# Expert weight parts: the load of part n+1 issued ahead of the stores of part n

## Chip, core and metric

The kernel runs on one core of one Trainium2 chip. The metric is device time in microseconds (us) for one execution. All engines of the core (TensorE, VectorE or DVE, ScalarE or ACT, GpSimd or POOL, SyncE or SP) run their own instruction streams and meet at semaphores.

## The reference

Four layers run one after the other on 3125 nodes of 256 features, each added to its input:

```python
x = x + gcn(_layernorm(x), edges, edge_weight, ...)     # 2 GCN layers
x = x + moe(_layernorm(x), ...)                         # 8 experts, top 2 of each token
x = x + ggnn(_layernorm(x), edges, edge_weight, ...)    # 5 rounds of message passing and a GRU
x = x + ffn(_layernorm(x), ...)                         # 8 experts, 2 chosen for all
```

There are 50000 edges. In a GCN layer a node sums the rows of its neighbours, weighted by the edges; the expert layer of the second line is what the change touches:

```python
xe = xn[None, :, :] * ln_g[:, None, :] + ln_b[:, None, :]
h = gelu(einsum('end,edh->enh', xe, W1) + b1[:, None, :])      # W1: 8 x 256 x 1024
y = einsum('enh,ehd->end', h, W2) + b2[:, None, :]             # W2: 8 x 1024 x 256
```

## The kernel before

**Dense planes.** The sparse sums are made dense. The kernel holds two matrices of 3200 x 3200 in device memory, `plane_a` (for the GCN) and `plane_w` (for the GRU rounds). They are filled with zeros (and ones on the diagonal of `plane_a`), and the edges are added to them by scatters of GpSimd with accumulation: 392 per plane, each of 128 edges. For `plane_a` they go in 28 batches of 14 (`NB`, `G`; L495 to L499, called from the loop at L508). A batch starts only when the one before has landed (L515); from batch 9 on, one scatter into `plane_w` (L501 to L505) is issued at its head. When the 28 batches are out, GpSimd goes on with `plane_w` alone, up to 252 of its 392, and does the rest between the gathers of the MoE layer.

**Split weights.** TensorE computes in a format of reduced precision, so each operand is given as a rounded high half and the rest as a low half, and a product takes three matmuls (L605). The weights of the first expert layer are brought into this form early: 16 parts (`PARTS`), W1 and W2 of 8 experts, each part 128 partitions x 2048 fp32 (1 MB). SyncE loads a part into `part_in` (`load_part`, L341 to L345), ScalarE rounds it into `part_hi` (`round_part`, L951 to L955), VectorE subtracts to get `part_lo` (`rest_of_part`, L1383 to L1387), and SyncE stores both halves to `w_split` in device memory (L356 to L358). All three buffers have two places, taken by n % 2. `round_part` waits for the load (`part_got`) and, from n = 2, for the stores of part n - 2 (`part_kept`); `part_l` counts finished splits, one for each part.

**The order around it.** SyncE's stream is written out by hand: zeros for `plane_w`, then at L347 the wait for all slots to be computed, the part loop (L348 to L360), a wait until all stores have landed (L361, L362), ten small loads of GCN and router weights (L363 to L369), the wait for all 392 scatters into `plane_a` (L370), and then the panels of `plane_a` for the GCN sweeps (L371 to L378; a panel is 5 tiles of 128 rows x 512 columns, three in flight). In the part loop stands a gate on the scatters: the stores of part n wait until BP + n // 2 = 18 + n // 2 batches have landed (L354). At n = P0 = 4 SyncE also stores five products for the GRU (`gru_v`, L350 to L353). ScalarE and VectorE do parts 0 to 3 (P0), then those products, the layernorm, the degree factors and the scaled node rows (`hs_ready`), and then parts 4 to 15, before they enter the GCN sweeps. In the sweeps ScalarE rounds a tile (L981), VectorE subtracts (L1415) and TensorE multiplies (L605).

The part loop before the change:

```python
sp.wait_ge(placed, NB + 2)
load_part(0)
for n in range(PARTS):
    ...
    sp.wait_ge(scat_a, 16 * G * (BP + n // 2))
    sp.wait_ge(part_l, n + 1)
    for x, half in enumerate((part_hi, part_lo)):
        sp.dma_start(w_split[...], half[:, n % 2, :] ...).then_inc(part_kept[n % 2], 16)
    if n + 1 < PARTS:
        load_part(n + 1)
```

Of the kernel before, what the change touches and what calls it, by code (L numbers as in the profile page):

```python
# [61 lines left out]
PARTS = 2 * X0  # L62
# [34 lines left out]
def build(nc, a, out):  # L97
# [11 lines left out]
    with ctx:  # L109
# [208 lines left out]
        def _(sp):  # L318
# [22 lines left out]
            def load_part(n):  # L341
                e, m = n // 2, n % 2
                src = (a["L0_ffn_W1"][e, :, :], a["L0_ffn_W2"][e, :, :])[m]
                k = (KD, H0 // 128)[m]
                sp.dma_start(part_in[:, n % 2, :].rearrange("p (k h) -> p k h", k=k), src.rearrange("(k p) h -> p k h", p=128)).then_inc(part_got[n % 2], 16)  # L345
# [3 lines left out]
            for n in range(PARTS):  # L349
                if n == P0:  # L350
                    for i in range(LAYERS):
                        sp.wait_ge(v_out, 4 * i + 4)
                        sp.dma_start(gru_v[i * D:(i + 1) * D, :].rearrange("(k p) g -> p k g", p=128), v_st[:, i % 2, :, :]).then_inc(v_kept[i % 2], 16)  # L353
                sp.wait_ge(scat_a, 16 * G * (BP + n // 2))  # L354
                sp.wait_ge(part_l, n + 1)
                for x, half in enumerate((part_hi, part_lo)):  # L356
                    sp.dma_start(w_split[n // 2, x, n % 2 * (PW // PC):(n % 2 + 1) * (PW // PC), :, :].rearrange("c p n -> p c n"),
                                 half[:, n % 2, :].bitcast(FP32).rearrange("p (c n) -> p c n", n=PC)).then_inc(part_kept[n % 2], 16)  # L358
                if n + 1 < PARTS:
                    load_part(n + 1)  # L360
            for b in range(2):  # L361
                sp.wait_ge(part_kept[b], 32 * X0)  # L362
            for l in range(2):  # L363
# [7 lines left out]
            for q in range(2 * GCH):  # L371
                c = q % GCH
                for r in range(NT // RB):
                    n = NT // RB * q + r
# [1583 lines left out]
```

## Time and profile before

| | us |
|---|---|
| median of 3 timed runs | 3883.78 |
| lowest, highest | 3877.94, 3884.19 |
| the profiled execution | 3878.37 |
| its span, first to last instruction | 3876.7 |

| engine | busy us | share of the span |
|---|---|---|
| TensorE (PE) | 3047.4 | 79% |
| its weight loads (PEld) | 2749.4 | 71% |
| VectorE (DVE) | 2376.2 | 61% |
| ScalarE (ACT) | 1530.8 | 39% |
| GpSimd (POOL) | 1410.5 | 36% |

The shares are means over stages with different limits: edges and scatters up to some 930 us, the GCN sweeps to some 1450, the MoE layer to some 1950, the GRU rounds to some 3650, the last layer to the end. DMA instructions count as GpSimd's work while it writes their descriptors; SyncE's issues stand in the timeline as SPq. "Idle before" and the name behind the arrow say how long an engine stood still ahead of an instruction, and whose end released it.

### The profile page before, as it was taken

Reading aid. Unit: us, or ns where it says so; the run is one execution under the profiler, and the core shown is the slowest. Engines: PE = TensorE matmul, PEld = TensorE weight load, DVE = VectorE, ACT = ScalarE, POOL = GpSimd, SP = SyncE. Lnnn points to the kernel's source line nnn. Section 1 sums busy time; section 2 is a strip of 40 time slices with the busy share of each in tenths; the row PEclk is TensorE's granted clock in tenths of the full one; section 3 lists DMA queues with packets and bytes.
Section 4 is the critical chain, followed back from the end, with each engine's and each line's share of the span. In section 5 each row is a group of like instructions: output and inputs, shape, how many; then the busy total and the mean of one; then the engine's idle time right before and its main releaser. Section 6 shows DMA issues by size and latency. Waiting matters only on the chain.

```text
span 3876.7 us, 54544 instructions
## 1 busy us (share of the span) xinstructions
PE 3047.4 (79%) x18100; PEld 2749.4 (71%) x18101; DVE 2376.2 (61%) x5044; ACT 1530.8 (39%) x3100; POOL 1410.5 (36%) x921
## 2 busy tenths in 40 slices
PE   2455454200999994999959999999999999999788
PEld 2444453100888893888848988998998898899677
DVE  7999995511777876555565555455545555555447
ACT  2344342111444552333334444444444444444255
POOL 1577888887777772878800000000000000000000
PEclk9999998655999996999979999999999999999889
DMA  9877334577667665435264433343433343343100
GB/s 394 265 226 196 38 48 86 127 207 206 177 163 200 180 150 169 128 94 136 34 207 140 131 118 128 119 131 116 133 128 119 127 131 121 126 131 131 37 31 28
DMA packets 378075, 538.46 MB, mean 139 GB/s; under 512 B 125780, under 2 KB 283643, under 8 KB 374459
## 3 DMA queue, kind: packets, MB, share of 16 engines
q1 hardware_dynamic: 251076, 487.82, 37.1%
q0 software_dynamic: 119088, 19.33, 8.5%
q10 hardware_dynamic: 7750, 29.17, 2.1%
q8 instruction: 100, 1.64, 0.2%
q14 instruction: 61, 0.49, 0.0%
HBM read 398.99 MB, written 137.25 MB: 138 GB/s over the span
## 4 chain that ended last, share of the span: by engine, by line
PE 44%; DVE 4%; ACT 1%; DMA 1%; issue 0%; SPq 0%; POOL 0%; ACTq 0%; DVEq 0%
PE bank L605 43%; DVE ring_lo L1700 1%; PE bank L784 1%; PE bank L853 1%; DMA yg_end<-chosen 0%; DVE gates_sb L1726 0%; ACT ring_hi L1105 0%; DVE gates_sb L1725 0%; DVE res_b L1812 0%; DVE xT L1727 0%; DVE v_lo L1757 0%; DVE stats L1778 0%; DVE stats L1815 0%; DVE nat L1787 0%; DVE res L1762 0%
## 5 line engine op out<-in xcount | busy, mean ns | idle before, releaser
L504 POOL DMA_INDIRECT plane_w<-pair,slot x392 | 655.5, 1672 | 184.1 <-issue 126.4
L498 POOL DMA_INDIRECT plane_a<-pair,slot x392 | 622.4, 1588 | 258.4 <-issue 123.4
L605 PE MATMUL bank<-ring_hi,h_hi 128*128 128x448 f32 x1750 | 653.6, 373 | 57.4 <-DVE ring_lo L1700 52.0
L1700 DVE TENSOR_TENSOR ring_lo<-ring_lo,ring_hi 128x448 fp32r<-128x448 f32 x875 | 521.8, 621 | 219.0 <-ACT ring_hi L1105 218.7
L1105 ACT ACTIVATE ring_hi<-ring_lo 128x448 fp32r<-128x448 f32 x875 | 497.2, 576 | 384.6 <-PE bank L605 377.8
L605 PE MATMUL bank<-ring_lo,h_hi 128*128 128x448 f32 x1750 | 643.6, 368 | 0.0
L605 PE MATMUL bank<-ring_hi,h_lo 128*128 128x448 f32 x1750 | 643.4, 368 | 0.0
L552 POOL DMA_DIRECT2D v_lo<-gru_v x5 | 3.6, 724 | 1382.8 <-PE bank L605 1308.3
L605 PE MATMUL bank<-gring_hi,hs_hi 128*128 128x512 f32 (+2 forms) x700 | 262.3, 375 | 243.5 <-DVE gring_lo L1415 243.5
L605 PEld LDWEIGHTS bank<-ring_hi,h_hi 128*128 128x128 f32 x1750 | 332.1, 190 | 84.9 <-DVE h_lo L1767 45.8
L1718 DVE SCALAR_TENSOR_TENSOR gates_sb<-bank,bhh,gates_sb 128x448 f32<-128x448 f32 x70 | 47.9, 684 | 516.4 <-ACT gates_sb L1129 516.4
L605 PEld LDWEIGHTS bank<-ring_hi,h_lo 128*128 128x128 f32 x1750 | 331.8, 190 | 26.8
L605 PEld LDWEIGHTS bank<-ring_lo,h_hi 128*128 128x128 f32 x1750 | 332.5, 190 | 24.8
L605 PEld LDWEIGHTS bank<-gring_hi,hs_hi 128*128 128x128 f32 x700 | 132.8, 190 | 265.3 <-issue 244.0
L577 PE MATMUL bank<-parts,eq 128*128 x392 | 58.2, 169 | 326.7 <-DVE hit_hi L1359 304.7
L981 ACT ACTIVATE gring_hi<-gring_lo 128x512 fp32r<-128x512 f32 (+2 forms) x350 | 199.6, 584 | 268.4 <-PE bank L605 160.5
L1415 DVE TENSOR_TENSOR gring_lo<-gring_lo,gring_hi 128x512 fp32r<-128x512 f32 (+2 forms) x350 | 207.5, 629 | 110.6 <-ACT gring_hi L981 106.2
L577 PEld LDWEIGHTS bank<-parts,eq 128*128 128x128 bf16 x392 | 39.1, 105 | 330.2 <-issue 330.2
L928 ACT ACTIVATE off_lo<-row,dlo_neg 128x128 f32<-128x128 f32 x392 | 151.7, 387 | 301.0 <-DVE hit_hi L1359 259.8
L605 PE MATMUL bank<-gring_lo,hs_hi 128*128 128x512 f32 (+2 forms) x700 | 257.9, 368 | 0.0
L605 PE MATMUL bank<-gring_hi,hs_lo 128*128 128x512 f32 (+2 forms) x700 | 257.8, 368 | 0.0
L1128 ACT ACTIVATE gates_sb<-bank,brz 128x448 f32<-128x448 f32 x70 | 44.5, 635 | 473.8 <-PE bank L605 473.8
(349 smaller groups left out, 6737.2 us busy)
## 6 DMA issues: line engine op xcount, KB each, us to landing
ring_lo<-plane_w SPq DMA_DIRECT2D x175, 1120.0 KB, 5.4
gring_lo<-plane_a SPq DMA_DIRECT2D x50, 1280.0 KB
plane_a<-nat SPq DMA_DIRECT2D x25, 1600.0 KB, 43.3
plane_w<-nat SPq DMA_DIRECT2D x100, 400.0 KB
w_hl<-w_split SPq DMA_DIRECT2D x16, 2048.0 KB
part_in<-in_L_ffn_W SPq DMA_DIRECT2D x16, 1024.0 KB
w_split<-part_hi SPq DMA_DIRECT2D x16, 1024.0 KB, 4.4
w_split<-part_lo SPq DMA_DIRECT2D x16, 1024.0 KB, 7.8
```

Of the source, the lines that this page charges most:

```text
L498: g_.indirect_dma_start(out=plane, out_offset=bass.IndirectOffsetOnAxis(slot[:, t:t + 1], 0), in_=pair[:, k, t:t + 1], in_offset=None, com ...
L504: g_.indirect_dma_start(out=plane_w, out_offset=bass.IndirectOffsetOnAxis(slot[:, n:n + 1], 0), in_=pair[:, 0, n:n + 1], in_offset=None, c ...
L577: mm(ps_sum[c][:, g, :], eq_row(c, g, g, g + 1), parts(g, 8), start=True, stop=(g == G - 1))
L605: last = mm(ps, lhs[x], rhs[y], start=start and n == 0, stop=stop and n == 2)
L784: last = tr(turned_tile(i, t)[:, k * 128:(k + 1) * 128], xT[:, k, t * 128:(t + 1) * 128], ident[:, :])
L928: A(off_lo[:, g % 2, :], row[:, :], ACT.Square, bias=dlo_neg[:, bass.ds(n * G + g, 1)]).then_inc(lo_apart, 1)
L981: A(gring_hi[:, n % RH, 0:w_], gring_lo[:, n % RS, 0:w_].bitcast(FP32), ACT.Copy).then_inc(ring_h, 1)
L1105: A(ring_hi[:, t % HS, :], ring_lo[:, t, :].bitcast(FP32), ACT.Copy).then_inc(hi_rdy, 1)
L1128: A(gr[:, j, :], gate_ps[0][:, 0:GW], ACT.Sigmoid, bias=brz[:, j:j + 1])
L1415: V.tensor_tensor(gring_lo[:, n % RS, 0:w_], gring_lo[:, n % RS, 0:w_].bitcast(FP32), gring_hi[:, n % RH, 0:w_].bitcast(FP32), ALU.subtrac ...
L1700: V.tensor_tensor(ring_lo[:, t, :], ring_lo[:, t, :].bitcast(FP32), ring_hi[:, t % HS, :].bitcast(FP32), ALU.subtract).then_inc(lo_rdy, 1)
L1718: link(V.scalar_tensor_tensor(gr[:, j, :], gate_ps[3][:, 0:GW], bhh[:, 2 * KD + j:2 * KD + j + 1], gr[:, j, :], ALU.add, ALU.mult))
```

## The change

```diff
--- before.py
+++ after.py
@@ -351,13 +351,15 @@
                     for i in range(LAYERS):
                         sp.wait_ge(v_out, 4 * i + 4)
                         sp.dma_start(gru_v[i * D:(i + 1) * D, :].rearrange("(k p) g -> p k g", p=128), v_st[:, i % 2, :, :]).then_inc(v_kept[i % 2], 16)
+                if n + 1 < PARTS:
+                    if n > 0:
+                        sp.wait_ge(part_l, n)
+                    load_part(n + 1)
                 sp.wait_ge(scat_a, 16 * G * (BP + n // 2))
                 sp.wait_ge(part_l, n + 1)
                 for x, half in enumerate((part_hi, part_lo)):
                     sp.dma_start(w_split[n // 2, x, n % 2 * (PW // PC):(n % 2 + 1) * (PW // PC), :, :].rearrange("c p n -> p c n"),
                                  half[:, n % 2, :].bitcast(FP32).rearrange("p (c n) -> p c n", n=PC)).then_inc(part_kept[n % 2], 16)
-                if n + 1 < PARTS:
-                    load_part(n + 1)
             for b in range(2):
                 sp.wait_ge(part_kept[b], 32 * X0)
```

In SyncE's stream the load of part n + 1 moves from behind the stores of part n to ahead of the two waits of part n. From n = 1 it waits for `part_l` at n, that is until part n - 1, the last user of its place in `part_in`, has been split. Nothing else is changed.

## Rows read from the trace of the kernel before

**Rows 1.** Page, 40 slices of the span (96.9 us each), busy tenths.
```profile
PE   2455454200999994999959999999999999999788
...
POOL 1577888887777772878800000000000000000000
```

**Rows 2.** Timeline, all engines, 935 to 975: start, us, engine, line, operation, idle before.
```profile
946.26 0.37 SPq L365 DMA_DIRECT2D gw<-in_L_gnn_W  x1
...
951.06 20.89 SPq L377 DMA_DIRECT2D gring_lo<-plane_a  x4
...
960.31 2.71 ACT L981 ACTIVATE gring_hi<-gring_lo 128x512 fp32r<-128x512 f32 x5 [23.92 <-DMA gring_lo<-plane_a]
...
961.88 0.76 PE L605 MATMUL bank<-gring_hi,hs_hi 128*128 128x512 f32 x1 [238.10 <-DVE gring_lo L1415]
...
963.80 1.67 ACT L981 ACTIVATE gring_hi<-gring_lo 128x512 fp32r<-128x512 f32 x3 [0.78 <-DMA gring_lo<-plane_a]
```

**Rows 3.** Timeline of POOL, 925 to 960: the end of the scatters into plane_a.
```profile
930.45 1.55 POOL L498 DMA_INDIRECT plane_a<-pair,slot  x1 [0.30 <-issue]
...
937.86 2.28 POOL L504 DMA_INDIRECT plane_w<-pair,slot  x1 [0.30 <-issue]
...
954.25 1.55 POOL L504 DMA_INDIRECT plane_w<-pair,slot  x1 [4.85 <-DMA plane_w<-pair,slot]
```

**Rows 4.** Waits of SP's queue: us in total, times, longest.
```profile
SPq L355 <- DVE part_lo L1387: 239.4, 16, 43.7
SPq L357 <- DMA plane_a<-pair,slot: 2.4, 7, 0.4
```

**Rows 5.** Timeline of SP's queue, 600 to 1040: the part loop.
```profile
643.06 0.40 SPq L345 DMA_DIRECT2D part_in<-in_L_ffn_W  x1
...
768.39 0.37 SPq L357 DMA_DIRECT2D w_split<-part_hi  x1
...
769.35 1.12 SPq L345 DMA_DIRECT2D part_in<-in_L_ffn_W  x1
...
938.79 0.36 SPq L357 DMA_DIRECT2D w_split<-part_hi  x1
```

**Rows 6.** Stretches: us, PE, PEld, DVE, ACT, POOL busy (count), PEclk, DMA, GB/s.
```profile
652.50:663.90 11.40, 0.00 (x0) 0.00 (x0) 0.00 (x0) 0.06 (x1) 9.57 (x7) 0.54 0.97 276
663.90:668.10 4.20, 0.00 (x0) 0.00 (x0) 2.29 (x1) 1.85 (x1) 3.59 (x3) 0.50 0.27 0
```

**Rows 7.** Timeline of ACT, 630 to 1000: rounding of part 0.
```profile
648.24 1.91 ACT L955 ACTIVATE part_hi<-part_in 128x2048 fp32r<-128x2048 f32 x1 [6.11 <-DMA part_in<-in_L_ffn_W]
```

**Rows 8.** Timeline of DVE, 630 to 1000: the low half of part 0.
```profile
650.18 2.29 DVE L1387 TENSOR_TENSOR part_lo<-part_in,part_hi 128x2048 fp32r<-128x2048 f32 x1 [7.15 <-ACT part_hi L955]
```

**Rows 9.** Timeline of POOL, 800 to 960: first scatters of two late batches.
```profile
842.46 1.55 POOL L498 DMA_INDIRECT plane_a<-pair,slot  x1 [1.55 <-DMA plane_a<-pair,slot]
844.31 2.90 POOL L498 DMA_INDIRECT plane_a<-pair,slot  x1 [0.30 <-issue]
...
904.41 1.55 POOL L498 DMA_INDIRECT plane_a<-pair,slot  x1 [1.59 <-DMA plane_a<-pair,slot]
```

**Rows 10.** Stretches, columns as in group 6: four stages.
```profile
150.00:361.00 211.00, 106.36 (x1346) 100.26 (x1346) 204.23 (x595) 89.26 (x295) 155.72 (x101) 1.00 0.79 233
384.00:634.30 250.30, 125.58 (x1584) 118.57 (x1582) 240.90 (x696) 102.27 (x338) 209.11 (x136) 1.00 0.32 37
751.00:932.30 181.30, 0.00 (x0) 0.00 (x0) 38.63 (x40) 19.09 (x10) 150.06 (x91) 0.50 0.71 188
1516.00:1946.00 430.00, 395.58 (x2622) 356.72 (x2622) 235.63 (x456) 144.07 (x230) 333.27 (x252) 0.97 0.42 102
```

**Rows 11.** Timeline of POOL, 176 to 184: a batch without a scatter into plane_w.
```profile
182.24 1.55 POOL L498 DMA_INDIRECT plane_a<-pair,slot  x1 [2.14 <-DMA plane_a<-pair,slot]
```

**Rows 12.** Timeline of POOL, 1461 to 1518: the first gather of the MoE layer.
```profile
1516.55 1.02 POOL L523 DMA_INDIRECT xT<-tokens,idx_x  x1 [51.07 <-DVEq L1629]
```

**Rows 13.** Waits of all engines, 630 to 965: ACT for the loads of parts.
```profile
ACT part_hi L955 <- DMA part_in<-in_L_ffn_W: 220.9, 15, 38.3
```

## Prediction

> **What bounds the kernel now.** I read the page's slices first. The GCN sweeps keep TensorE at 9 tenths or more from about 970 us on; in the slices from 700 to 960 TensorE is nearly empty and POOL runs at 8 tenths [rows 1]. The question is therefore what holds back the first matmul of the sweeps, and the timeline of all engines across that point answers it [rows 2]: TensorE's first matmul (961.88) comes after 238.10 us of idling and waits for DVE, DVE for ACT (960.31), and ACT for the first panel of `plane_a`, which SyncE issues at 951.06. SyncE issues it the moment the ten small loads of L365 to L369, the first at 946.26, are out, and those begin when the last two stores of `w_split`, issued from 938.79 on [rows 5], have landed. The only other condition on the panel is L370, that all 392 scatters into `plane_a` have landed. The last of them leaves POOL at 930.45 + 1.55 = 932.00 [rows 3], so that wait is over by some 935 and costs nothing today. SyncE's own program is the later of the two, by about 16 us.
>
> Why SyncE is late shows in its waits and its timeline [rows 4, 5]. L355 waits 239.4 us in 16 times for `part_lo`; the gate of L354 appears at most in the 2.4 us put down to `plane_a`. From part 4 (stores at 768.39) to part 15 (938.79) a part takes 170.40 / 11 = 15.49 us. Within one period the table of stretches separates two phases [rows 6]: for 11.4 us the DMA engines are 0.97 busy (two stores of 1024 KB, then the load behind them), and for 4.2 us they are at 0.27, while ACT rounds for 1.91 us and DVE subtracts for 2.29 us [rows 7, 8]. The load of a part is issued behind the stores of the part ahead of it, although its buffer has been free all along.
>
> **Part by part.** *The load goes ahead of the stores.* There is no new instruction but one wait, and 16 loads and 32 stores remain. On SyncE the order becomes load n+1, [gates], stores n. Load n+1 thus follows the stores of n-1 directly: it is issued a whole iteration earlier. Its new wait (`part_l` at n) asks for what the stores of n-1 have waited for already, so nothing queued behind it on SyncE (the gate of L354, the stores) stands longer. At n = 4 the `gru_v` stores of L353 stay ahead of load 5, but load 4 now leaves ahead of them with part 3. Its 1.12 us of issue [rows 5] lies in the wait for `part_lo`.
>
> *The period.* The split of one part can now lie under the transfers of the next, and what is left is DMA time. Its upper bound is the whole busy stretch, 11.4 us. The lower bound: that stretch holds one latency that overlaps too; a 1024 KB load alone takes 648.24 - 643.06 = 5.18 us from issue to use [rows 5, 7], and as panels of 1280 KB issued together follow each other by 963.80 - 960.31 = 3.49 us [rows 2], some 5.18 - 2.8 = 2.4 us of it is latency, so 9.0 us. I take 10.5, nearer the upper, since the scatters share the engines.
>
> *Where part 15 ends.* If part 4 is split no sooner than now, its stores leave at 768.39 and those of part 15 at 768.39 + 11 x 11.4 = 893.8; with 10.5, at 883.9. Parts 0 to 3 also shorten, which pulls the layernorm and part 4 forward; this only widens the cushion. The gates are older than that: part 14 asks for 25 batches of scatters, complete at 842.46 [rows 9]. Adding the 7.5 us from the last stores to the first small load (938.79 to 946.26) and 4.8 us for the ten of them, SyncE reaches L370 at 906 at the latest, against 951.06.
>
> *What is late next.* The wait at L370 now counts: all scatters landed. So SyncE's gain of 45 us is cut off at the end of the scatters. Their time is POOL's: a batch of 14, plus one scatter into `plane_w`, takes 250.3 / 9 = 27.8 us in the quiet stretch from 384.0 to 634.3 (nine such batches by the count of instructions, 136) and 181.3 / 6 = 30.2 us from 751.0 to 932.3, beside the parts (91 instructions) [rows 10]. Two kinds of row explain the difference [rows 9]. Each `part_lo` stretches one scatter (2.90 us for 1.55 at 844.31, about the most), and at a batch's end, behind the one `plane_w` scatter that covers it, POOL may idle 1.55 us instead of 0.30 until the batch has landed.
>
> *What the change does to POOL.* The stretch by DVE comes once a part wherever it lies; of 16, only part 15's fell behind the last `plane_a` scatter (in the `plane_w` one at 937.86, 2.28 us for 1.55 [rows 3]), so one more counts: 0.7 us, or up to 1.35. The batch ends: today four of those beside the parts show the extra 1.25 us (842.46 and 904.41 are two of them [rows 9]). With the queue full, six ends lie in the loaded time up to 895, so 2 x 1.25 = 2.5 us more. Together 3 us. The bounds: 0 (the last two batches run free of parts and gain back what the others lose) and 13, if a landing takes at all six ends the 4.85 us that the uncovered one at 954.25 shows behind small loads and panels [rows 3]: covered by 1.85 us of the `plane_w` scatter, less the usual 0.30, that is 6 x 2.7 = 16.2, less the 5 now paid, and 1.35 for the split.
>
> The Trainium skill has a rule that speaks against the change: by "DMA: Bandwidth & Descriptors", section "Queues, rings and completion order", each DMA engine takes turns between the queue rows that have work, a whole packet at a time, so a scatter's packets would wait longer once SyncE's row never runs empty. By that rule POOL's batch ends would lengthen, by the sum above the whole way to 13 us. The trace bears out the turn-taking only mildly: at 0.79 busy (150 to 361 us) an end without a covering scatter idles 2.14 us, and at 0.71 the landing behind a cover takes 1.55 + 1.85 = 3.4 us [rows 9, 10, 11].
>
> *From the last scatter to the first matmul.* Last issue over at 932.0 + 3 = 935.0. Landing: 2.14 us by the uncovered end at 182.24 [rows 11] (3.4 if it were loaded; it no longer is); so L370 opens at 937.1, and the panel is issued. It took 9.25 us from there to ACT's first rounding (951.06 to 960.31), but that included the small loads ahead of it in the queue, long done after the change. A lone load took 5.18 us; with 256 KB more, 5.9 us. I take 5.9, with 9.25 as the other end. First rounding at 943.0 instead of 960.31: **a gain of 17.3 us**.
>
> *What lies behind.* All that follows is released by this start and shifts with it, if nothing else holds. POOL goes through the `plane_w` scatters and then idles 51.07 us until the token indices are there at 1516.55 [rows 12]; it is delayed by 3 and asked for 17 earlier, so 31 us of cover remain. TensorE is idle before the sweeps as now: the granted clock is 0.50 of full (1.2 GHz) from 751 to 932 and the first matmul lasts 0.76 us [rows 2, 10]; its warming up moves along unchanged. If POOL's cover were gone, each further us would be lost at the MoE.
>
> **Sum.** Profiled execution: 3878.37 - 17.3 = 3861.1 us (span 3876.7 to 3859.4, 1.7 around it). The three timed runs have their median at 3883.78, 5.4 above it; from that, 3883.78 - 17.3 = **3866.5 us**, my forecast.
>
> **Rivals.**
> (a) *The scatters pay.* The mechanism of the 13 us bound: gain (951.06 - 932.0 - 13 - 2.1) + 0 to 3.3 = 4 to 7.3 us (3.3 = 9.25 - 5.9), so 3876.5 to 3879.8. It is what the rule cited above comes to (the Trainium skill, "DMA: Bandwidth & Descriptors", "Queues, rings and completion order"). For it: 4.85 us at 954.25. Against: the loaded stretch from 652.5 is already at 0.97 [rows 6], and loaded ends like 842.46 cost only 1.55. 0.12.
> (b) *No overlap.* The parts keep near 15.5 us, or the gain is under the point that decides: SyncE beats the scatters only if part 15 is stored by 937.1 - 12.3 = 924.8, a period under (924.8 - 768.39) / 11 = 14.2 us. If the DMA engines, not the order, set 15.5, the time stays at 3883.8. Against: 0.27 busy in 4.2 us of each period. 0.04.
> (c) *Given back later.* Beyond the sweeps, `plane_w` scatters, gathers and the experts share POOL, which is busy for 333.27 of 430 us from 1516 [rows 10] and loses 0.30 us ahead of each of 252 instructions, 409 us in all; were the `plane_w` scatters slowed in the sweeps by over 31 us, or the landings there met otherwise, half of the gain could go: 3875. 0.06.
> (d) *Slower.* A batch must land before the next one may start. If SyncE's full queue held landings back far more than any row shows, the sweeps would begin later than now. The point from which it decides: a delay of the scatters of 17.3 + 3 + 7.8 = 28.1 us, so (28.1 + 5 - 0.7) / 6 = 5.4 us at each of six ends beyond 0.30, a landing in 1.85 + 0.3 + 5.4 = 7.5 us. At 8 us the delay is 6 x 5.85 - 4.3 = 30.8, the time 3883.8 + 30.8 - 20.3 = 3894. The longest landing between scatters that I found is the 4.85. 0.03.
>
> **How the numbers follow.** Forecast 0.75 (gain 12 to 21.3: the upper end with no extra scatter time and 5.2 us to the first rounding), (a) 0.12, (b) 0.04, (c) 0.06, (d) 0.03. The bound of 0.2% is 7.8 us, about what a measurement of this kernel can tell from no change. Over it: the forecast and the better half of (c) and some of (a) with a smaller loss: 0.83. Within: the rest of (a), (c) and (b): 0.13. Slower: (d), and what I cannot name, 0.04. The range: 3883.78 less 6 gives 3878 at the top; at the bottom the best gain on the profiled execution, 3878.37 - 21.3 = 3857. It leaves out most of (a), (b) and (d).
>
> **What would show it.** In the profile after: stores of parts 4 to 15 some 9 to 11.4 us apart and the last before 895; DMA share over 0.9 in that stretch; ACT's wait for `part_in` well down from 220.9 us [rows 13]; SyncE waiting some 30 us ahead of L377 for `plane_a`'s scatters, last issued at 930 to 936; the first panel's rounding near 943; the MoE's first gather 17 us earlier. I am wrong if the last `plane_a` scatter ends after 940, if a part still takes over 14 us, or if the first gather has not moved with the sweeps.

## The result and the profile after

| | before | after |
|---|---|---|
| median of 6 timed runs each, us | 3883.99 | 3870.88 |
| lowest, highest | 3877.94, 3890.27 | 3867.37, 3879.76 |
| the profiled execution | 3878.37 | 3872.27 |
| its span | 3876.7 | 3870.7 |

The ratio of after to before is 0.9975, with a 95% interval of 0.9965 to 0.9985: 9.7 us faster, between 5.8 and 13.6. It is not the quotient of the two medians, which lie 13.1 us apart. A second series, of seven runs of the changed kernel, gave 0.9971 (0.9960 to 0.9982), or 11.3 us. The forecast was 17.3 us faster and 3866.5 us.

SyncE's queue in the changed kernel, first its waits (us in total, times, longest), between 620 and 1000 us; before, this was [rows 4]:

```profile
SPq L359 <- DVE part_lo L1389: 119.6, 13, 43.0
SPq L379 <- DMA plane_a<-pair,slot: 65.1, 1, 65.1
...
SPq L361 <- DMA plane_a<-pair,slot: 37.2, 6, 15.8
```

The wait for the subtraction is halved, and 65.1 us of waiting for the scatters into `plane_a` now stand ahead of the first panel. The timeline of the same queue answers [rows 5]:

```profile
769.76 0.36 SPq L361 DMA_DIRECT2D w_split<-part_hi  x1
...
777.91 0.36 SPq L361 DMA_DIRECT2D w_split<-part_hi  x1
...
798.25 0.36 SPq L361 DMA_DIRECT2D w_split<-part_hi  x1
...
829.60 0.36 SPq L361 DMA_DIRECT2D w_split<-part_hi  x1
...
861.08 0.36 SPq L361 DMA_DIRECT2D w_split<-part_hi  x1
...
862.10 1.04 SPq L361 DMA_DIRECT2D w_split<-part_hi  x1
...
874.48 0.37 SPq L367 DMA_DIRECT2D gw<-in_L_gnn_W  x1
...
944.34 92.66 SPq L379 DMA_DIRECT2D gring_lo<-plane_a  x14
```

Where nothing but DMA holds them, the parts follow each other by 8.15 us (769.76 to 777.91; the neighbouring two periods are 9.13 and 8.64) instead of 15.49. Parts 10, 12 and 14, at 798.25, 829.60 and 861.08, wait for the gate on landed batches. The stores of part 15 leave at 862.10, 77 us earlier than before. Yet the first panel leaves only 6.7 us earlier, at 944.34 for 951.06. The sweeps start from it (all engines, 944 to 952, the answer to [rows 2]):

```profile
950.23 2.19 ACT L983 ACTIVATE gring_hi<-gring_lo 128x512 fp32r<-128x512 f32 x4 [98.15 <-DMA gring_lo<-plane_a]
...
951.80 0.76 PE L607 MATMUL bank<-gring_hi,hs_hi 128*128 128x512 f32 x1 [251.19 <-DVE gring_lo L1417]
```

That is 10.1 us earlier than 960.31 and 961.88. In the second trace the rounding starts at 950.61. What holds the panel is POOL; its timeline in the changed kernel, with the three long waits for landings, one stretched scatter and the last scatter into `plane_a`:

```profile
670.41 1.55 POOL L500 DMA_INDIRECT plane_a<-pair,slot  x1 [4.56 <-DMA plane_a<-pair,slot]
...
744.15 2.21 POOL L500 DMA_INDIRECT plane_a<-pair,slot  x1 [0.30 <-issue]
...
762.42 1.55 POOL L500 DMA_INDIRECT plane_a<-pair,slot  x1 [4.60 <-DMA plane_a<-pair,slot]
...
798.68 1.55 POOL L500 DMA_INDIRECT plane_a<-pair,slot  x1 [5.23 <-DMA plane_a<-pair,slot]
...
941.33 1.55 POOL L500 DMA_INDIRECT plane_a<-pair,slot  x1 [0.30 <-issue]
```

The last scatter is issued by 941.33 + 1.55 = 942.88, against 932.00 [rows 3]. At three batch ends POOL waits 4.6 to 5.2 us, and at a fourth (700.09) 1.08 us, where before it waited 1.59 at most [rows 9]. So the change removed SyncE from the path and gave part of it to POOL: 10.9 us later scatters.

### The profile page after: what moved, and what is told of

Its sections match the earlier page's. It is cut to its first block, busy times and chain, and to the rows that moved or that the text cites. A ratio compares the mean times of both kernels' runs of the same rounds, so it can differ in the third digit from the quotient of the medians.

```text
span 3870.7 us, 54544 instructions
## 1 busy us (share of the span) xinstructions
PE 3051.9 (79%) x18100; PEld 2747.6 (71%) x18101; DVE 2375.8 (61%) x5044; ACT 1530.7 (40%) x3100; POOL 1414.4 (37%) x921
## 4 chain that ended last, share of the span: by engine, by line
PE 44%; DVE 4%; DMA 1%; ACT 1%; issue 0%; SPq 0%; POOL 0%; ACTq 0%; DVEq 0%
PE bank L607 43%; DVE ring_lo L1702 1%; PE bank L786 1%; PE bank L855 1%; DMA yg_end<-chosen 0%; DVE gates_sb L1728 0%; ACT ring_hi L1107 0%; DVE gates_sb L1727 0%; DVE res_b L1814 0%; DVE xT L1729 0%; DVE v_lo L1759 0%; DVE stats L1780 0%; DVE stats L1817 0%; DVE nat L1789 0%; DMA past_res<-chosen 0%
```

## The experiments

The same sum was made for every trace: over all scatters from batch 18 (which begins near 634) to the last one into `plane_a`, the time by which they last longer than 1.55 us ("stretch"), and the time by which the idling ahead of them exceeds 0.31 us ("waits"). The end of the last scatter less the start of batch 18 is 277.6 to 277.7 us plus these two, in all fourteen traces; for before 932.00 - 634.30 = 297.7 = 277.7 + 15.0 + 5.0. Nothing else moves POOL there. A kernel with one run has one trace and one time; its whole time does not separate it from its neighbours, and it is read by the place of its scatters.

| kernel | waits | stretch | last scatter ends | first panel | median (its series' before) |
|---|---|---|---|---|---|
| before | 5.0 | 15.0 | 932.0 | 951.1 | 3883.99 |
| before_again | 7.3 | 14.9 | 933.1 | 952.4 | 3882.55, one run |
| after | 14.2 | 17.1 | 942.9 | 944.3 | 3870.88 (3883.99) |
| after_again | 10.7 | 20.0 | 943.4 | 944.8 | 3869.72 (3881.30) |
| small_stores | 5.0 | 16.1 | 932.0 | 933.4 | 3855.19, one run |
| narrow_split | 12.4 | 5.1 | 928.4 | 929.9 | 3853.97, one run |
| no_gate | 15.1 | 14.1 | 941.6 | 943.0 | 3871.81, one run |
| late_only | 12.8 | 14.4 | 938.9 | 940.3 | 3859.86, one run |
| late_only_timed | 12.0 | 15.6 | 939.3 | 940.6 | 3867.85 (3879.34) |
| paced | 8.2 | 19.5 | 940.4 | 941.8 | 3864.18 (3881.30) |
| paced2 | 3.9 | 22.4 | 936.8 | 938.3 | 3864.41 (3879.60) |
| paced3 | 4.1 | 23.6 | 938.5 | 939.9 | 3866.51 (3879.60) |
| paced4 | 0.8 | 24.9 | 936.0 | 937.4 | 3863.39 (3879.34) |
| paced_quarters | 1.8 | 4.5 | 917.4 | 918.8 | 3846.86 (3882.94) |

In every kernel with the change the panel leaves 1.3 to 1.5 us behind the last scatter, in the two traces of before 19 us behind it. That the scatters' end is the new bound is thereby shown: it was moved between 917 and 943 and the panel went with it.

**after_again** is the changed kernel once more.

> The changed kernel once more, for its trace and its scatter. By the first trace of it the last scatter into plane_a ends at 942.88 us (932.00 before), with 14.2 us of idling for landings beyond the usual 0.30 and 17.1 us by which scatters are stretched; the first panel is issued at 944.34. Theory L (the full queue holds back the landing of a batch whose end it meets): the same again within 2 us in these places, median 3866 to 3875. If the 10.9 us of delay were chance, the last scatter would end near 935 here.

The last scatter came at 943.4, so the delay is no chance; the waits were 3.5 us less and the stretch 2.9 us more. The median was 3869.72, the ratio 0.9971.

**before_again** is the kernel before once more.

> The kernel before once more, for a second trace of it. The distances between stages show what changes from execution to execution: last plane_a scatter at 932, first rounding at 960.3, first gather 556.2 us behind it, first load of v_lo 506.5 us behind that, each within 2 us; the whole within 6 us of 3878.

The last scatter came at 933.1 and the rounding at 961.42, both a little late. The first gather followed 554.96 us behind the rounding and the first load of `v_lo` 506.03 us behind that, as expected. The execution took 3882.55; where the 4 us to the first trace arose stands in the last section.

**small_stores** takes nearly all of the stores of parts 4 to 15, two thirds of their traffic, away and leaves VectorE's work (a second edit, not shown, makes the expert layer read expert 0's weights for every expert):

```diff
+                    if n >= P0:
+                        sp.dma_start(w_split[n // 2, x, n % 2 * (PW // PC), :, 0:64], half[:, n % 2, 0:64].bitcast(FP32)).then_inc(part_kept[n % 2], 16)
+                        continue
```

> The changed kernel with the stores of parts 4 to 15 cut to 64 columns each; left out: the split weights of experts 2 to 7 are not kept, and all experts use those of expert 0. Loads, roundings and subtractions stay. Theory L: without two thirds of the queue's work the waits for landings behind part 4 go (9 us), the stretched scatters stay (some 17 us in all): last scatter at 933 to 935. Theory P: 942 as before, as the subtractions are all there.

Waits 5.0 and last scatter 932.0, one us below the expected span. Most of these 5.0 us is a wait of 4.26 us near 669, in the range of parts 0 to 3, whose stores are whole. Of the waits behind part 4 one of 1.32 us is left (POOL's timeline):

```profile
759.66 1.55 POOL L503 DMA_INDIRECT plane_a<-pair,slot  x1 [1.32 <-DMA plane_a<-pair,slot]
```

So the long waits come from what SyncE's queue holds, not from VectorE.

**narrow_split** is the opposite: all DMA, and from part 4 on hardly any subtraction.

```diff
+                c = PW if n < P0 else 64
-                V.tensor_tensor(part_lo[:, n % 2, :], part_in[:, n % 2, :], ...)
+                V.tensor_tensor(part_lo[:, n % 2, 0:c], part_in[:, n % 2, 0:c], ...)
```

> The changed kernel with the subtraction of VectorE cut to 64 columns for parts 4 to 15; left out: most of the low halves of these parts are stale. DMAs stay. Theory L: the waits for landings stay at some 14 us or change by their phase only, the stretch of the scatters falls from 17 to some 5 us: last scatter at 930 to 934. If the long waits for landings came from the subtractions, they would go as well: last scatter at 921 to 925.

The waits stayed (12.4, one of 4.06 us at 791.53), the stretch fell to 5.1, and the last scatter came at 928.4, somewhat earlier than expected. The two causes are separate.

**late_only** undoes the change for parts 0 to 3 alone.

```diff
-                if n + 1 < PARTS:
+                if P0 <= n and n + 1 < PARTS:
...
+                if n < P0:
+                    load_part(n + 1)
```

> One part of the change undone: for parts 0 to 3 the load is issued behind the stores as before, for parts 4 to 15 ahead of them. Theory L: the batch end near 664 costs nothing, as in the kernel before (instead of 4.3 us), the one near 692 1.2 us. Part 4 is split near 766 instead of 744; the parts behind it follow each other by some 8.5 us, meet the batch ends near 781 and 812 with a full queue and pay some 4.5 us at each: last scatter at 938 to 942. Should all loss of the changed kernel come from parts 4 to 15, it would be 943.

The wait near 664 was gone, as in the kernel before, the last scatter came at 938.9, and the two ends near 781 and 817 cost 4.98 and 4.86 us, a third 2.55. The last scatter is some 4 us earlier than in the changed kernel, but by the table this can't be put down to the wait of parts 0 to 3: the waits are 12.8 us in sum against 14.2 and 10.7 in the two traces of the changed kernel, since the later ends cost more here, and the larger part of the 4 us is less stretch (14.4 against 17.1 and 20.0). It was timed in a second run:

> late_only once more, timed. Its first trace had the last scatter at 938.9 and the panel at 940.29, against 936.8 and 938.25 in paced2. By the place of the panel it should lie 4 us below the changed kernel and 2 us above paced2: median 3864 to 3868; the 3859.86 of its single run would then be the low end of the scatter from one execution to the next.

Median 3867.85 (ratio 0.9963, 0.9950 to 0.9976), in the span expected; the single 3859.86 lies below all five of these runs (lowest 3861.22). The interval overlaps that of the changed kernel.

**no_gate** leaves the gate out.

> The changed kernel without the gate on landed batches. Parts 4 to 15 then follow each other by some 8.5 us from 745 to 840, with the queue full throughout. Theory L: three batch ends lie in that time (near 756, 792, 828) instead of two, at 4.3 to 5 us each, with the two of parts 0 to 3 some 18 us of waits for landings instead of 14.2 (10.7 in the second trace); last scatter at 945 to 949, SyncE done by 860. Were the delay a matter of the amount of DMA work alone, which is the same, it would stay at 943.

A miss in the sum. The third end did meet a loaded queue, but cost only 2.45 us, the waits came to 15.1 instead of 18, and the stretch happened to be 3 us less than in the changed kernel. The last scatter came at 941.6, not 945 to 949. By itself this run does not tell the theories apart.

**paced, paced2, paced3, paced4** change the gate alone:

```diff
-                sp.wait_ge(scat_a, 16 * G * (BP + n // 2))
+                sp.wait_ge(scat_a, 16 * G * (BP + n // 2 + (n >= P0)))                                # paced
+                sp.wait_ge(scat_a, 16 * G * (BP + n // 2 + 2 * (n >= P0)))                            # paced2
+                sp.wait_ge(scat_a, 16 * G * (BP + n // 2 + 2 if n >= P0 else BP + 1))                 # paced3
+                sp.wait_ge(scat_a, 16 * G * (BP + n // 2 + 2 if n >= P0 else BP + (n > 0)))           # paced4
```

> The changed kernel with one more batch in the gate of parts 4 to 15 (19 + n // 2 landed batches instead of 18 + n // 2). Theory L: each pair of parts then starts right behind the start of a batch, its some 20 us of DMA are over before the batch of 28 us ends, so the two waits of 4.3 and 4.9 us for landings in the range of parts 4 to 15 go; part 15 is stored by 905, still ahead of the scatters, and the last scatter ends at 932 to 935 instead of 943: median 8 to 10 us below the changed kernel, 3859 to 3864. Theory P (the delay is the sum of the port and of DMA work, wherever it lies): last scatter at 943 as in the changed kernel, median the same. Theory E (something behind the sweeps takes back what the sweeps win): last scatter early, median no lower than 3868.

The direction came true, the size only by a third (last scatter 2.5 to 3 us earlier): I had miscounted a batch, parts 4 and 5 still left at 744 to 746, late in a batch, and the wait at 761.53 stayed at 4.64. The end near 792 was free. The median went 5.5 us below the changed kernel of the same series (8 to 10 expected), more than the panel moved (3 us), which is within what medians of five to seven runs scatter.

> The changed kernel with the gate of parts 4 to 15 at 20 + n // 2 landed batches, so that parts 4 and 5 start with the batch that begins at some 755 and not late in the one before. Theory L (landings wait only where a batch's end meets the full queue): the wait of 4.6 us at 762 goes, only the one near 670 (4.1) stays among the long ones; last scatter at 935 to 937 against 940.4 in paced and 943 in the changed kernel. The last two parts are released at some 905 and their four stores have landed by 920, so SyncE is at L372 near 925, still ahead; median 3 to 5 us below paced, 3858 to 3862. If the period of the parts mattered and not their phase, the last scatter would stay at 940.

Only the wait of 4.21 us near 669 was left and the last scatter came at 936.8, as expected of landings. The median (3864.41, ratio 0.9963) was 2 us above the expected span and does not separate from that of paced.

> paced2, and the gate of parts 0 to 3 at 19 landed batches, so that the stores of parts 0 and 1 leave at some 664, behind the end of a batch, and not at 652 and 655. Theory L: the wait of 4.1 us at 670 goes; but the stores of parts 0 to 3 then come within one batch, some 30 us of DMA, and the next end (693) may pay instead. Last scatter between 931 and 937; median equal to paced2 or up to 4 us less.

The wait moved instead of going: 4.36 us at 700.6, the case named as its risk. Last scatter 938.5.

> paced2 with the gate of parts 1 to 3 at 19 landed batches: the stores of part 0 leave at 652, those of part 1 only behind the batch that ends near 664. Theory L: the end at 664 costs about 1.3 us instead of 4.2, and the stores of part 3 have landed just before the end near 693, which costs 0.3 to 1.3; last scatter at 934 to 937 with the usual 2 us for where the subtractions fall. If the end near 693 meets the queue full, it pays 4.3 there as paced3 did at 700.6, and nothing is won on paced2.

All waits but one of 1.10 us were gone, 0.8 us in sum. The last scatter came at 936.0 and no earlier, since the stretch had risen to 24.9. So the waits are a matter of phase: the same stores and loads cost 14 us or 1, by whether they are under way when a batch ends. The whole time of paced4 (ratio 0.9960, 0.9948 to 0.9971) does not separate from those of paced, paced2 and paced3.

What makes the stretch is seen by laying VectorE's timeline (first row) beside POOL's, in paced4:

```profile
806.47 2.29 DVE L1389 TENSOR_TENSOR part_lo<-part_in,part_hi 128x2048 fp32r<-128x2048 f32 x1 [6.84 <-ACT part_hi L957]
```
```profile
805.07 1.55 POOL L500 DMA_INDIRECT plane_a<-pair,slot  x1 [0.30 <-issue]
806.92 3.27 POOL L500 DMA_INDIRECT plane_a<-pair,slot  x1 [0.30 <-issue]
```

The scatter that starts at 805.07, ahead of the subtraction, lasts 1.55 us although they overlap by 0.15. The one that starts in it ends at 810.19, 1.43 us behind the subtraction's end at 808.76. In before, after and paced2 I laid all 48 subtractions beside POOL: each scatter that started within one ended 1.42 to 1.44 us behind its end (1.46 to 1.47 for the first of two back to back, whose end is taken at half of the pair), and none that started ahead of it was held by it, not even one that ran beside it for 1.36 of its 1.55 us (889.65 in before). The subtraction itself took 2.29 us each time. Some 1.4 us of each trace's stretch are not of the parts: they are 0.1 to 0.2 us at each of several scatters beside `hs_lo` and its neighbours. The Trainium skill ("GPSIMD Engine Reference", "Key points") says that GpSimd shares its SBUF interfaces with VectorE and contends with DVE instructions that have two SBUF inputs; this subtraction has two, and the trace agrees. The same timelines show one part of the rise to 24.9: in the changed kernel three of the 16 subtractions (665.80, 758.26, 792.62) ran while POOL waited for a landing and met no scatter, in paced4 each of the 16 met one. A hit costs 0.3 to 2.1 us in these traces, by where in the subtraction the scatter starts.

In the changed kernel two subtractions run back to back (VectorE's timeline):

```profile
742.65 4.49 DVE L1389 TENSOR_TENSOR part_lo<-part_in,part_hi 128x2048 fp32r<-128x2048 f32 x2 [0.22 <-DVE hs_lo L1408]
```

The scatter of 744.15 (2.21 us, shown with the result) ends at 746.36, 1.46 us behind the end of the first (742.65 and half of 4.49: 744.9). It slipped through between them. **paced_quarters** makes use of that, with the gate of paced4:

```diff
+                for c in range(4):
+                    at = slice(c * PW // 4, (c + 1) * PW // 4)
+                    last = V.tensor_tensor(part_lo[:, n % 2, at], part_in[:, n % 2, at], part_hi[:, n % 2, at].bitcast(FP32), ALU.subtract)
+                last.then_inc(part_l, 1)
```

> paced4 with each subtraction of VectorE cut into four of 512 columns. In all traces so far a scatter that starts while a part is subtracted ends 1.42 us behind the end of the subtraction, so it costs up to 2.16 us, and in paced4 that adds up to some 20 of the 24.9 us of stretch. Between two subtractions back to back (742.65 in the changed kernel) a scatter got through, ending 1.42 us behind the first of them. Theory S (only the start of a scatter is held, until the current DVE instruction ends): with pieces of 0.6 us a hit costs at most 0.5 us, the stretch falls to 6 to 10 us, the last scatter ends at 919 to 926, the panel is issued by 921 to 928 and the median is 10 to 16 us below paced4, 3848 to 3854. If it is the whole time of DVE's work that counts, the last scatter stays at 935 to 937.

The group of VectorE's instructions, then POOL's last scatter into `plane_a`, then SyncE's first panel:

```profile
L1391 DVE TENSOR_TENSOR part_lo<-part_in,part_hi x64: 678/685/736, 648.5 to 887.4; 128x512 fp32r<-128x512 f32 x64
```
```profile
915.84 1.55 POOL L500 DMA_INDIRECT plane_a<-pair,slot  x1 [0.30 <-issue]
```
```profile
918.76 1.52 SPq L379 DMA_DIRECT2D gring_lo<-plane_a  x3
```

The stretch fell from 24.9 to 4.5, below the expected 6 to 10, and the panel went 18.7 us ahead of paced4. The median is 3846.86, a little under the expected span, the ratio 0.9910 (0.9896 to 0.9924): 35 us below before by the ratio, over three times the gain of the change itself. It beats both kernels. VectorE's work does not get shorter by it (four pieces of 0.685 us, overlapping, take 2.50 in all, for 2.29); only what waits behind it does.

## Why the prediction was right or wrong, point by point

- **What bounds the kernel before**: right. SyncE's part loop held the first panel; with it gone the panel stands at the last scatter. The panel of the two traces of before came 19 us behind the last scatter, as read.
- **The period of the parts**: the direction was right, the size wrong. Forecast 10.5 us with 9.0 as the lower bound; the three ungated ones took 9.13, 8.15 and 8.64, and without the gate (no_gate, 759.76 to 836.41 for nine parts) the mean was 8.5. The lower bound took one latency off the busy stretch, but that stretch was not yet full either: in the changed kernel the table of stretches shows more data in the same time (columns as in [rows 6]).

```profile
745.00:811.00 66.00, 0.00 (x0) 0.00 (x0) 15.89 (x7) 12.68 (x7) 48.25 (x29) 0.50 1.07 346
```

  346 GB/s, where [rows 6] has 276. With parts that fast the gates, forecast as slack, became binding at parts 10, 12 and 14. SyncE's own lateness cost the path nothing by it, since it was ready 65 us early (forecast: some 30); what the gates do to the path goes by the phase of the transfers, as the paced kernels show.
- **From the stores to L370**: 12.4 us to the first small load (862.10 to 874.48) for a forecast of 7.5, since parts 14 and 15 are stored together (in no_gate, which stores them apart, it was 7.5: 836.41 to 843.88); hidden.
- **What the change does to POOL**: this is the term that was mis-sized. Forecast 3 us, between 0 and 13; measured 932.0 to 942.9 = 10.9, and 11.4 in the second trace. By the sum: waits 14.2 for 5.0 (9.3 more), stretch 17.1 for 15.0 (2.0 more), batch 18 begins 0.3 earlier. I had counted six loaded ends at 1.25 us each, four of them paid already. Only three met the full queue and a fourth just the edge of it, but the three cost 4.56, 4.60 and 5.23 us: a landing of 1.85 + 5.23 = 7.1 us, longer than the 4.85 that I took as the far end. I carried a price over from batch ends behind which the queue was running dry to ends in a queue that was still full. The bound of 13 held by luck: too many ends stood against too low a price; rival (d) named 7.5 us at all six as its point of decision, and three of them came near it.
- **The skill's rule**: the rows show the landing behind a cover growing from 3.4 us to 6.4 to 7.1 us when SyncE's queue is full, and small_stores shows that it goes with that queue's content. By the rule cited in the prediction (the Trainium skill, "DMA: Bandwidth & Descriptors", "Queues, rings and completion order") the engines take turns between rows by whole packets; the trace agrees that landings lengthen beside a full row, and I had given it too little weight. That the turn-taking is what lengthens them no run shows apart. The outcome lies between the forecast's case (a gain of 12 to 21.3) and rival (a) (4 to 7.3), nearer (a) in its mechanism.
- **The stretch by VectorE**: forecast one hit more (0.7 us); measured 2.0. The count was wrong: "once a part wherever it lies" does not hold when POOL waits. Up to the last scatter into `plane_a` there were 15 hits before (13.6 us) and 13 after (15.6 us), since three subtractions fell into the waits for landings. The price of a hit rose instead, from 0.91 to 1.20 us in the mean; it depends on where the subtraction falls against the scatters, which the change shuffled. In the second trace 15 hits cost 18.7 us. No run was made to say why the price rose; its share in the 10.9 us is luck of the phase as far as is known.
- **From the last scatter to the rounding**: right. Landing by 1.46 us (forecast 2.14), panel to rounding 5.89 us (forecast 5.9).
- **What lies behind**: right in that it shifted along. POOL's idling ahead of the first gather went from 51.07 [rows 12] (45.56 in the second trace of before) to 23.6 us (forecast 31), because it is done with its `plane_w` scatters 16 us later:

```profile
1505.31 1.03 POOL L525 DMA_INDIRECT xT<-tokens,idx_x  x1 [23.61 <-DVEq L1631]
```

  The gather is 11.2 us earlier in the first trace, 9.3 in the second. The end of the first profiled execution is only 6.0 us earlier, that of the second 9.9; the difference of 5.2 arose behind the gather, 3.0 of it in the first GRU round (329.3 to 332.3), where the executions of one kernel differ as much (last section).
- **The rivals**: (b) did not occur. (c) did not occur; nothing was given back beyond the spread of executions.
- **The sum**: 17.3 less 7.9 for POOL, plus 0.7 for the landing, is 10.1 us for the first rounding, and the ratios give 9.7 and 11.3. The median of 3870.88 lies in the range of 3857 to 3878, but the case that the range was built on, a gain of 12 to 21.3 us (the sum for its upper end gives 21.0), did not come about; the range held because its top was set by going 6 us under the time before, and not by that case. The forecast of "faster by over 0.2%" held in the ratio, with an interval whose end (0.15%) lies within the bound.
- **The signs named beforehand**: one of the three of being wrong came true. The last `plane_a` scatter ended at 942.9 and 943.4, after the 940 named. A part did not take over 14 us: from part 4 to part 15 it was 117.09 / 11 = 10.6 us in the mean, near the forecast 10.5 by chance, out of shorter periods and the gates' waits; the first gather moved with the sweeps. The last store came before 895 (863), ACT's waits for `part_in` fell from 220.9 to 138.6 us, and the DMA share was over 0.9 up to 811 only, for the gates then spread the parts. So the forecast is right in its direction, its path and its range, and wrong in what the scatters pay.

## What to carry to other kernels

When a wait is taken off one engine, the work behind it moves into the time of whatever becomes late next; price it by rows in which that resource is loaded without a pause, not by rows at the edge of such a stretch, and count how many of the critical engine's waits fall into it. Bulk transfers beside latency-bound ones held up least here when released right behind a point of synchronization, so that they were over before the next (waits of 0.8 us for 14.2). A long two-input VectorE instruction beside GpSimd's scatters cost less here when it was cut into pieces.

## What the runs showed of the hardware

A scatter of GpSimd that starts while VectorE subtracts ends some 1.42 us after that instruction, whatever its start; pieces of 0.685 us instead of 2.29 took the sum from 24.9 to 4.5 us. I had seen the stretch, but not that it depends on the start alone. An accumulating scatter's landing behind a covering one took 3.4 us beside one part at a time and 6.4 to 7.1 us in the changed kernel, at ends where SyncE's queue was still full.

The six timed executions of before lie up to 12.3 us apart, those of after 12.4. Of the two traced ones of each kernel, 4.2 and 3.8 us apart, much of the difference lies in one place: from the first load of `v_lo` to the second (one GRU round) it took 329.3 and 334.2 us in the two traces of before, 332.3 and 328.7 in those of after, and 327.4 to 334.0 in the others. Stretches of 40 us in this round show it (columns as in [rows 6]): in the first trace of after, then in the second.

```profile
2080.00:2120.00 40.00, 40.00 (x196) 36.32 (x195) 18.29 (x29) 16.91 (x30) 0.00 (x0) 1.00 0.35 115
```
```profile
2080.00:2120.00 40.00, 40.00 (x200) 37.07 (x199) 19.43 (x31) 16.95 (x29) 0.00 (x0) 1.00 0.38 119
```

TensorE is busy throughout, at a granted clock of 1.00 in both, and does 196 matmuls in the one and 200 in the other. What sets the slower pace stays open; it comes with either kernel, so no difference of some 6 us between the whole times of single executions is put down to a change here.
